# Gate tiles regrouped and unread products added on TensorE in a delta-rule recurrence

## What is computed

```python
def step(S, xs):
    q_t, k_t, v_t, a_t, b_t = xs
    Sk = jnp.einsum('bhvk,bhk->bhv', S, k_t)
    S = a_t[..., None] * S - (b_t[..., None] * (Sk - v_t))[..., None] * k_t[:, :, None, :]
    o_t = jnp.einsum('bhvk,bhk->bhv', S, q_t)
    return (S, o_t)
...
g = jax.nn.sigmoid(x @ Wg.T).reshape(B_, T_, H, DV)
o = (o * g).reshape(B_, T_, H * DV)
return o @ Wo.T
```

## Time and profile before

| | |
|---|---|
| three runs | 2413.17 us median (2405.32 to 2416.09) |
| profiled execution | 2418.26 us, span 2416.5 us |
| TensorE busy | 2105.1 us, 87% |
| VectorE busy | 1895.8 us, 78% |
| ScalarE busy | 1238.9 us, 51% |
| mean granted TensorE clock | 0.912 of full |

### The profile page before, as it was taken

The page is one execution under the profiler, slowest core; times in us unless marked ns, Lnnn a source line. Parts: engine busy times, 40 slices in busy tenths (PEclk is TensorE's granted clock), DMA queues, the critical chain, the costliest instruction groups (busy, mean ns, idle before and its releaser), DMA issues.

```text
span 2416.5 us, 61545 instructions
## 1 busy us (share of the span) xinstructions
PE 2105.1 (87%) x21890; PEld 1602.9 (66%) x21890; DVE 1895.8 (78%) x4382; ACT 1238.9 (51%) x2692; POOL 521.8 (22%) x577
## 2 busy tenths in 40 slices
PE   6999999999995888887888887888888888866999
PEld 4444888888874766775766766667667667753566
DVE  4222799999995888987978978888988988987776
ACT  3000587787782555654645645555555545533332
POOL 0000144444442211211121221121221211222000
PEclk9999999999996888988888888988988888877999
DMA  7000177777779556555556655556566555566540
GB/s 262 9 9 9 62 260 264 268 268 264 266 266 336 200 184 209 208 198 201 202 186 214 207 193 200 197 191 221 195 199 213 180 179 200 193 210 260 199 157 18
DMA packets 229473, 468.45 MB, mean 194 GB/s; under 512 B 48432, under 2 KB 172328, under 8 KB 199640
## 3 DMA queue, kind: packets, MB, share of 16 engines
q1 hardware_dynamic: 226184, 454.06, 53.9%
q10 hardware_dynamic: 2976, 10.72, 1.2%
q0 software_dynamic: 48, 0.16, 0.0%
HBM read 316.36 MB, written 149.57 MB: 193 GB/s over the span
## 4 chain that ended last, share of the span: by engine, by line
PE 45%; DVE 28%; issue 16%; ACT 5%; DMA 4%; DVEq 1%; POOL 1%; ACTq 1%; SPq 0%; POOLq 0%
DVE arena L1066 10%; PE PS L1503 7%; PE PS L1662 5%; PE PS L1517 4%; PE PS L1489 3%; PE PS L1372 3%; PE PS L1581 3%; PE PS L1542 3%; DVE arena L1157 3%; DVE arena L1172 3%; DVE arena L1165 2%; PE PS L1445 2%; PE PS L1395 2%; DVE arena L1149 2%; PE PS L1530 2%
## 5 line engine op out<-in xcount | busy, mean ns | idle before, releaser
L1395 PE MATMUL PS<-arena 128*128 x2048 | 463.7, 387 | 1.8 <-DVEq L1051 1.0
L1066 DVE SCALAR_TENSOR_TENSOR arena<-PS,SM,arena 128x256 f32<-128x256 f32 x1152 | 452.9, 478 | 15.5 <-ACT arena L721 15.5
L1395 PEld LDWEIGHTS PS<-arena 128*128 128x128 f32 x2048 | 383.8, 188 | 81.7 <-DVE arena L1066 6.5
L1503 PE MATMUL PS<-arena 128*128 128x128 f32 x1920 | 321.8, 318 | 38.4 <-ACT arena L860 36.7
L1503 PEld LDWEIGHTS PS<-arena 128*128 128x128 f32 x1920 | 271.5, 219 | 77.9 <-ACT arena L860 55.6
L627 POOL TENSOR_TENSOR arena<-arena 128x256 f32<-128x256 f32 x128 | 114.9, 897 | 914.2 <-DVE arena L1172 914.2
L852 ACT ACTIVATE arena<-arena 128x128 f32<-128x128 f32 x960 | 306.7, 395 | 0.0
L721 ACT ACTIVATE arena<-PS,SM 128x256 f32<-128x256 f32 x384 | 209.5, 564 | 89.3 <-PE PS L1395 84.3
L1111 DVE TENSOR_TENSOR arena<-arena,PS 128x512 f32<-128x512 f32 x192 | 127.5, 685 | 116.5 <-PE PS L1542 112.5
L1489 PE MATMUL PS<-ident,arena 128*128 128x128 f32 x960 | 180.4, 320 | 27.2 <-ACT arena L852 26.1
L1517 PE MATMUL PS<-arena 32*128 32x128 f32 x1920 | 173.5, 330 | 25.7 <-DVE arena L1100 18.0
(11 more groups left out here) (135 smaller groups left out, 3212.5 us busy)
## 6 DMA issues: line engine op xcount, KB each, us to landing
arena<-g_d SPq DMA_DIRECT2D x126, 1024.0 KB, 5.6
arena<-vas_d SPq DMA_DIRECT2D x124, 384.0 KB, 3.2
vas_d<-arena SPq DMA_DIRECT2D x32, 1024.0 KB, 11.4
kq_d<-arena SPq DMA_DIRECT2D x8, 4096.0 KB, 11.5
arena<-kq_d SPq DMA_DIRECT2D x14, 2048.0 KB, 7.9
arena<-beta_d SPq DMA_DIRECT2D x8, 2048.0 KB, 9.2
kb_d<-arena SPq DMA_DIRECT2D x8, 2048.0 KB, 10.3
vas_d<-arena SPq DMA_DIRECT2D x8, 2048.0 KB, 12.4
```

What stands on the lines that cost most here:

```text
L1066: nc.vector.scalar_tensor_tensor(acc, raw[:, :, i:i + PT_], CW[:, w, i, hh:hh + 1], acc, ALU.mult, ALU.add).then_inc(job_free if i == TAPS ...
L1395: ins = mm(dst.rearrange("p (b n) -> p b n", b=B), W4[:, w, kt, DH * h:DH * (h + 1)], XNT[:, kt, :, bass.ds(c * PT_ + (HALO - halo), halo ...
L1503: ins = mm(bank(7)[:, 128 * gi:128 * (gi + 1)].rearrange("v (l x) -> v l x", l=NB), STR[:, s % 2, gi, :], KQ[d][:, :, p0:p0 + 2].rearrange ...
```

## The change

Four things change, all in the recurrence.

1. In the early chunks three of the four gate tiles stay in block 0 of the chunk, and the fourth is computed after the reads of block 2, ahead of that block's correction transposes. `GATE_HEAD` gives the tiles' order: the first comes from `WGA`, the second and third from `WGB`, the fourth from `WGA`.
2. `WGB` is loaded from ScalarE's queue, once the first half of `carried` is done, in place of SyncE's queue once both halves are.
3. The fourth sigmoid stands in block 3 on ScalarE; its store and the next load of `WGA` (and of `XG`) stand at the end of block 2 on SyncE. The waits on banks 6 and 7 are adapted.
4. `keep_awake` takes the bank as an argument, and in each of the 15 chunks that have a next one it also issues four unread products at the end of block 5's reads and preparations and three at the end of block 7's, into bank 6. The three in block 0 of the chunks without gate tiles stay.

```diff
+GATE_HEAD = [0, 2, 3, 1]
...
             def chunk(n, i, c, nxt, nxt2, early):
+                def store_gate(k):
+                    it, q = early
+                    sp.wait_ge(early_gate, n * 4 + k + 1)
+                    lo = CH * (4 * q + GATE_HEAD[k])
+                    sp.dma_start(gate_d[bass.ds(it, 1), :, lo:lo + CH].rearrange("c v x -> (c v) x"), GST[k]).then_inc(early_stored[k], 16)
+
                 if early:
-                    it, q = early
-                    sp.wait_ge(corr_full, n * 9 + 2)
-                    sp.dma_start(WGB, wg_v[:, :, DH * (4 * q + 2):DH * (4 * q + 4)]).then_inc(wgb_in, 16)
-                    for k in range(4):
-                        sp.wait_ge(early_gate, n * 4 + k + 1)
-                        lo = CH * (4 * q + k)
-                        sp.dma_start(gate_d[bass.ds(it, 1), :, lo:lo + CH].rearrange("c v x -> (c v) x"), GST[k]).then_inc(early_stored[k], 16)
-                        if k == 1:
-                            load_wga((q + 1) % 4)
-                    if q == 3:
-                        load_xg(it * -128 + (128 * (NCH - 2) + HALO))
+                    for k in range(3):
+                        store_gate(k)
...
+                    if m == 2 and early:
+                        store_gate(3)
+                        load_wga((early[1] + 1) % 4)
+                        if early[1] == 3:
+                            load_xg(early[0] * -128 + (128 * (NCH - 2) + HALO))
...
+                    def gate_tile(k):
+                        act.wait_ge(early_psum, n * 4 + k + 1)
+                        nc.scalar.activation(GST[k], bank(6 + k % 2), ACT.Sigmoid).then_inc(early_gate, 1)
+
                     if m == 0 and early:
-                        for k in range(4):
-                            act.wait_ge(early_psum, n * 4 + k + 1)
+                        q = early[1]
+                        act.wait_ge(corr_full, n * 9 + 1)
+                        act.dma_start(WGB, wg_v[:, :, DH * (4 * q + 2):DH * (4 * q + 4)]).then_inc(wgb_in, 16)
+                        for k in range(3):
                             if k == 2:
                                 act.wait_ge(r_stored, n * 128 + 64)
-                            nc.scalar.activation(GST[k], bank(6 + k % 2), ACT.Sigmoid).then_inc(early_gate, 1)
+                            gate_tile(k)
                     if m == 1:
                         act.wait_ge(e_in[c], i * 16 + 16)
                     if reads:
                         decay(reads[0])
+                    if m == 3 and early:
+                        gate_tile(3)
...
+                    if s in (0, 4) and early:
+                        pe.wait_ge(early_gate, n * 4 + (2 if s == 0 else 4))
...
-                def early_gates():
-
-                    for k in range(4):
...
+                def early_gate_tile(k):
+
+                    if k == 0:
+                        pe.wait_ge(xg_in, early[0] * 16 + 16)
+                        pe.wait_ge(wga_in, n * 16 + 16)
+                    elif k == 1:
+                        pe.wait_ge(wgb_in, n * 16 + 16)
+                    elif k == 2:
+                        pe.wait_ge(early_gate, n * 4 + 1)
+                    elif k == 3:
+                        pe.wait_ge(x_read, 1 + n * 16 + 4)
+                    w, h = (WGA, WGB)[k in (1, 2)], GATE_HEAD[k] % 2
+                    for kt in range(2):
+                        ins = mm(bank(6 + k % 2), w[:, kt, DH * h:DH * (h + 1)], XG[:, kt, :], start=(kt == 0), stop=(kt == 1))
+                    ins.then_inc(early_psum, 1)
+
+                def keep_awake(count, b):
 
                     for _ in range(count):
-                        mm(bank(7), ident[:, :], PT32[:, 0:4].rearrange("r g v -> r (g v)"), start=True, stop=True)
+                        mm(bank(b), ident[:, :], PT32[:, 0:4].rearrange("r g v -> r (g v)"), start=True, stop=True)
...
                     if m == 0 and early:
-                        early_gates()
+                        for g in range(3):
+                            early_gate_tile(g)
                     elif m == 0 and nxt:
-                        keep_awake(3)
+                        keep_awake(3, 7)
...
                     for x in preps:
                         prep(m, *x)
+                    if nxt and m == 5:
+                        keep_awake(4, 6)
+                    elif nxt and m == 7:
+                        keep_awake(3, 6)
                     if m == NB - 1:
                         prep_taken(m)
+                    if m == 2 and early:
+                        early_gate_tile(3)
                     if m < NB - 1 or nxt:
                         corr_transposes(m)
```

More of the change, by code:

```diff
@@ L301, in build @@
         x_v = x_tm.rearrange("(n p) d -> p n d", p=128)
+        wg_v = wgT.rearrange("(c p) n -> p c n", p=128)
         def silu_of(x):
@@ L437, in _ @@
             sp.wait_ge(xnT_stored, 16)
-            wg_v = wgT.rearrange("(c p) n -> p c n", p=128)
             xn_v = xnT_d.rearrange("p (k b n) -> p k b n", k=2, b=B)
@@ L1494, in reads_of @@
                     pe.wait_ge(tr_ready, n * 16 + s + 1)
+                    if s in (0, 4) and early:
+                        pe.wait_ge(early_gate, n * 4 + (2 if s == 0 else 4))
                     if s == 0:
                         pe.wait_ge(kq_in[d], (i + 1 + c) * 16)
-                        if early:
-                            pe.wait_ge(early_gate, n * 4 + 4)
                     else:
```

13 lines of the change are left out of this document (removed).

## The result

| | before | after |
|---|---|---|
| median of 20 runs each, us | 2410.19 | 2427.82 |
| lowest to highest, us | 2400.72 to 2429.84 | 2410.05 to 2446.21 |
| ratio to before, 95% interval | | 1.0073 [1.0055, 1.0091] |
| profiled execution, us (its span) | 2418.26 (2416.5) | 2419.31 (2417.6) |

The forecast was 2391 us with a range up to 2425, so both sign and range were missed. So the traces tell where time went inside a chunk, and the medians tell what it sums to. Neither profile is a typical run, and the mean granted clock of the whole span shows it: 0.912 before and 0.931 after, where the median over the runs is 0.919 before (23 runs beside the first four experiments) and 0.925 after (20 runs).

A forecast was written before the change was run, and what follows sets the result against it. It took the kernel as bound by the hand-over between TensorE and VectorE in the recurrence, with TensorE's clock falling. -30 + 12 - 19 + 18 - 31 + 20 + 8 = -22 us gave a 2391 us median, range 2350 to 2425.

The forecast's parts named there:

- part 5: Blocks 0, 4 and 6: clock falls there shift as chunks reach their waits at other moments, +8 us (bounds -10 and +30).
- part 2: Block 2: fourth gate tile ahead of the correction transposes, +12 us of path; 70% of falls behind it go, -19 us.
- the falls move: Rival, chance 0.20: half the gain comes back in blocks 0, 4 and 6, or weights come late; 2408 us.
- the falls stay: Rival, chance 0.16: unread products lengthen the path and the clock falls all the same, a little later; 2433 us.
- Part 1: Block 0: three gate tiles in place of four in 12 chunks, and waits for weights gone, -30 us.
- -9.1, all waits gone: Block 0: with the second weight half issued early by ScalarE, all 9.1 us of waits for weights vanish.
- The upper bound: Block 0's worst case: weights land in 9.7 us each time, 3.4 us of new wait in 12 chunks, +41 us.
- The price of 2.7 us for a fall: Block 2's to block 3's correction products: 11.80 us with a clock fall, 9.06 us at full clock.
- Part 3: Block 5: four unread products in 15 chunks, +18 us of path; four in five falls behind them go, -31 us.
- Part 4: Block 7: three unread products in 15 chunks make the sixteen transposes 1.37 us late, +20 us.
- Nothing comes back: Block 7: no gain offsets its products, as no fall stands between them and the next chunk's start.
- the rival of the cleared head: Rival, chance 0.14: the clock also holds through the chunk's start, 1.6 us a chunk, no shifted falls; 2359 us.

The follow-up runs named there:

- the first four experiments: Gate tiles' move alone, unread products alone, the changed kernel without block 7's products, and without block 5's: 2406.38, 2427.40, 2407.14 and 2430.24 us.
- e2: The kernel before with only the unread products of blocks 5 and 7 added, four gate tiles staying in block 0: 2427.40 us, ratio 1.0089.
- A: The changed kernel without the unread products of blocks 5 and 7, so the moved gate tiles alone: 2406.38 us, ratio 0.9996 to the kernel before.
- e11: Moved gate tiles with short 128-column fills inside waits, one wide unread product in block 3 and two in block 5: 2376.46 us, ratio 0.9860.
- e14: e11 with the loads ScalarE issued between the first broadcast and the loop put on SyncE's queue: 2371.57 us, ratio 0.9861.
- B: The changed kernel without block 7's three unread products: 2407.14 us, ratio 1.0005 to the kernel before.
- e8: The changed kernel with two unread products in block 5 in place of four and none in block 7: 2398.53 us, ratio 0.9957.
- e5_narrow: The changed kernel with its seven added unread products using 32 rows in place of 128: 2508.18 us, ratio 1.0427.

## Why the prediction was wrong

**The step that failed is part 5**, "half a us a chunk" for falls that come elsewhere. In the kernel after, the stretches that it had at nothing cost 1.1 + 0.8 + 0.8 = 2.7 us a chunk, five times the term. 1.9 us of it are falls in new places, behind block 0 and in block 4; 0.8 us is VectorE's in block 3, an overlap that part 2 had wrong. In the kernel with the gates alone the same places have +1.3 and +3.1 us, 0.8 of it again without a fall; against that, blocks 4 to 7 are 2.5 us shorter. The forecast had counted falls as things at a place, each with a cause in the wait ahead of it. The traces show them coming in stretches where before had none: behind block 0 once a tile has left it (not in e2, where it stays), in block 3 in A, in block 4 once block 5 is filled. The sum went down all the same, from 20.5 to 15.2 us a chunk at the lower clock. Of the kernels that have the tiles moved, those that filled blocks 3, 5 and 6 and the short waits too (e11, e14) kept the most. Why a fall comes in one thin stretch and not in another no run shows. The rival "the falls move" named this mechanism, and was priced too low; "the falls stay" had the time nearly right (2433) for a reason that is wrong, since both falls it spoke of are gone.

**Part 1, block 0.** -1.77 a tile was right: the stretch is 2.2 us shorter, in spite of 1.25 us more at the lower clock. "-9.1, all waits gone" held in chunks 1 to 11 and was wrong by chunk 0, where the second tile now waits for weights, 8.8 us for its weight load and 7.4 us for its product, one wait that the first row counts twice:

```profile
  DMA arena<-wgT: 16.2, 2
...
  PEld PS L1592: 8.8, 1
  PE PS L1592: 7.4, 1
...
DMA to landing us min/median/max: 2.7/4.0/15.9
```

These are the answers to the earlier trace rows: median landing 4.0 us, the issue from ScalarE early as argued, but in one chunk 15.9, above the upper bound of 9.7 that I had taken from SyncE's queue. What stood ahead on the queue was to be read off the code and the sizes of the transfers: two broadcasts, three blocks of values, keys and queries of the second chunk, 6.5 MB. The 30.5 us to chunk 0's transposes are 9.0 more than before. In sum the part brought 2.19 x 11 - 9.0 = 15 us of the 30. (The upper bound itself was mis-added: 1.9 + 9.7 - 7.9 is 3.7 us a chunk and +44 us, not 3.4 and +41.)

**Part 2, block 2.** The path cost was right, +0.98 us. Of the falls behind block 2 all went in chunks 1 to 11, not seven in ten, and that stretch is 2.1 us shorter where 1.6 was forecast; but 0.8 us come back from block 3 to 4, where VectorE then bounds, so 1.3 us is what it is worth. The price of 2.7 us for a fall had been read from a stretch that ended too early. The tile's wait for ScalarE is the 0.46 us forecast:

```profile
1071.78 1.98 PE L1592 MATMUL PS<-arena 128*128 128x512 f32 x4 [0.46 <-ACT arena L872]
```

**Part 3, block 5.** The path cost was right and the clock's gain also (-3.0 for -2.6), and yet the part is worth -8 or +2 us and not -13. Block 4 has new falls, +0.8 us, and with the tiles moved there is less to win: block 5 to 6 is 12.88 us in A and 11.15 in B, 1.7 us less, against 2.4 us more from block 4 to 5. The products also delay block 5 by 1.7 us in each chunk where two of them, inside the wait, would not (e8, e11). That is the choice of a number, which I took from the change and didn't ask about.

**Part 4, block 7.** +20 us forecast, 16 to 27 measured. "Nothing comes back" held: no fall stood there. It is also the whole of the loss.

**The sum.** In the trace the forecast's -2.1 us a chunk came out at -0.43, which is +18 us in eleven chunks, and chunk 0 at +6.4 instead of -2.1, +8.5; chunks 12 to 14, which have no gate tiles, at -0.1 each instead of +1.0, -3: -22 + 18 + 8 - 3 = +1, and the two profiled executions differ by 1.1. The medians differ by 17.6. That the other 16 us are in falls too is borne out by the granted clock: it is 0.019 higher after in the two profiles, 0.006 in the medians of the runs, and over the 20 runs of the kernel after 0.001 less of it goes with some 2.2 us more. (In the rival of the cleared head, 24 us is 1.6 us in 15 chunks; gate tiles stand in 12, which gives 19 us and 2364.)

**The rule of that section.** The Trainium skill, "TensorE: Matmul & The Clock Gate", section "HAM oscillation — how this bites in real kernels", ties the fall to an idle gap longer than any wait that stands ahead of these falls. The runs disagree: filling waits of 0.5 to 1.8 us took away the falls of blocks 2 and 5, and e5_narrow, which fills the same waits for the same time, did not. And the fall of 0.70 above follows waits of 0.73 and 0.57 us.

**What stays open.** What the pause marked "issue" is: no row shows it, and it wasn't tried whether another length of the loop's body moves it. Why chunk 10 of e11 has it without a fall. In which blocks the runs of after that take 2440 us lose their time. And what about the fourth tile held off the fall behind block 0: no kernel put anything else in its place.

## What to carry to other kernels

Price a fall of the clock for the whole loop body, not for its place: before removing one, list every stretch with waits of half a us and small products, and expect a fall in others of them, also where full products have just been taken out. Ask how far the other engine ran ahead during the fall, since that part does not come back. Fill waits with products of all 128 rows, as many as the wait holds and not one more: what goes beyond the wait is on the path. And before a transfer is moved to another engine's queue, add up what that queue already holds at its first use.

## What was not expected of the hardware

- Rows count: products of 32 rows and 512 columns, as long and as many as those of 128 rows, did not hold the clock (block 5 to 6 15.4 us against 11.15; ratio 1.0427 against 1.0073).
- A fall can last: 21.4 us at a mean of 0.60 in block 3 of A. VectorE was busy 15.8 of these 21.4 us, against 12.5 of 13.3 at full clock, and TensorE 18.2 against 11.3, 85% of both: at half clock the others wait for it, and the stretch is no denser. Why it lasts no run shows.
- TensorE pauses, waiting for nothing shown, 1.5 to 2.3 us at one place of the loop's body, once per pass, in e11; a further one of 3.0 to 3.8 us stands at the first update of chunk 4, where the second pass begins, in before and after alike (1134.53 and 1134.97), and in before and e11 in that of chunk 8 too:

```profile
1134.97 2.08 PE L1528 MATMUL PS<-arena 32*128 32x128 f32 x16 [3.37 <-issue]
```
